# Scatter stage of a graph network kernel: GpSimd copies the next group's edge attributes in mid-group, in place of a wait for four scatters to land

## The reference

```
out_i = softplus(concat(x[i], edge_attr) @ W)      # (E, 4, 64)
out_j = softplus(concat(x[j], edge_attr) @ W)
alpha = softplus(sum(concat(out_i, out_j) * att))  # (E, 4)
alpha = softplus(batch norm of alpha over all edges)
alpha = softmax of alpha over the edges of one i
out   = mean over heads of segment_sum(out_j * alpha, i) + bias
x     = layernorm(x + out)
```

## Time and profile before

| | us |
|---|---|
| median of 3 runs | 7369.46 |
| lowest and highest | 7367.15, 7384.98 |
| the profiled execution, its own time | 7374.29 |
| the span of its profile | 7372.1 |
| mean granted TensorE clock | 0.861 |

### The profile page before, as it was taken

The page is one execution under the profiler, slowest core; times in us unless marked ns, Lnnn a source line. Parts: engine busy times, 40 slices in busy tenths (PEclk is TensorE's granted clock), DMA queues, the critical chain, the costliest instruction groups (busy, mean ns, idle before and its releaser), DMA issues. The chain is left out here.

```text
span 7372.1 us, 162457 instructions
## 1 busy us (share of the span) xinstructions
PE 5061.6 (69%) x33039; PEld 3158.5 (43%) x33040; DVE 5308.0 (72%) x27929; ACT 4071.5 (55%) x10690; POOL 2017.3 (27%) x2671
## 2 busy tenths in 40 slices
PE   1226766666666766637777777777724999995877
PEld 0113444344344443424444444444413555554877
DVE  5626666666666666629999999999987888887122
ACT  0015555455555555537777777777735889884000
POOL 0035555555655555541111111111100000000000
PEclk8557778778888778869999999999967999997978
DMA  4565555555555555555555555555514878773956
GB/s 33 219 226 166 178 165 177 169 165 178 170 177 168 171 174 164 172 175 144 144 145 145 144 146 144 144 145 145 144 34 121 214 213 222 213 214 103 381 225 258
DMA packets 905819, 1259.82 MB, mean 171 GB/s; under 512 B 267668, under 2 KB 774531, under 8 KB 884180
## 3 DMA queue, kind: packets, MB, share of 16 engines
q1 hardware_dynamic: 783812, 843.53, 41.2%
q0 software_dynamic: 88656, 333.99, 12.1%
q10 hardware_dynamic: 33216, 80.75, 3.2%
HBM read 832.07 MB, written 425.87 MB: 171 GB/s over the span
## 5 line engine op out<-in xcount | busy, mean ns | idle before, releaser
L840 POOL DMA_INDIRECT rows<-rowS,idx x1616 | 1605.0, 993 | 1151.7 <-DMA rows<-rowS,idx 605.1
L1530 DVE CUSTOM_DVE_ANT_1 junk<-bufh,attb 128x128 bf16<-128x128 f32 x7296 | 1693.7, 292 | 3.7 <-ACT bufh L1570 3.7
L1096 PE MATMUL psa<-one_c,one_s 128*128 128x392 bf16 x2352 | 651.4, 395 | 763.7 <-issue 322.7
L2219 PE MATMUL psm<-msg,onem 128*128 128x260 f32 x3648 | 1011.5, 402 | 135.1 <-issue 50.8
L989 ACT ACTIVATE lgS<-preS 128x1024 f32<-128x1024 f32 x404 | 412.7, 1021 | 893.0 <-remote 638.3
L2219 PEld LDWEIGHTS psm<-msg,onem 128*128 128x128 f32 x3648 | 619.1, 189 | 527.0 <-issue 473.0
L1502 POOL COPY eaC<-bufh 128x128 f32<-128x128 f32 x912 | 322.0, 353 | 1793.9 <-DMA bufh<-rows 1789.1
L923 DVE TENSOR_SCALAR one_c<-ioc,code 128x392 bf16<-128x392 f16 x2352 | 779.1, 331 | 18.3 <-DVE code L915 3.7
L1566 ACT ACTIVATE lg<-pre 128x512 f32<-128x512 f32 x912 | 544.9, 598 | 423.4 <-PE pre L1609 423.3
L2186 DVE TENSOR_TENSOR msg<-oj,alpha 128x512 f32<-128x512 f32 x912 | 631.1, 692 | 185.7 <-issue 96.7
L915 DVE TENSOR_SCALAR code<-pairS,codes 128x3 f32<-128x3 f32 x784 | 201.4, 257 | 782.2 <-remote 531.8
(11 more groups left out here) (275 smaller groups left out, 8107.7 us busy)
## 6 DMA issues: line engine op xcount, KB each, us to landing
bufh<-rows SPq DMA_DIRECT2D x912, 322.0 KB, 3.0
oj<-rows SPq DMA_DIRECT2D x912, 256.0 KB
adj<-adj SPq DMA_DIRECT2D x98, 1568.0 KB, 8.4
adj<-cnts ACTq DMA_DIRECT2D x49, 1568.0 KB
eaS<-in_edge_attr_dram SPq DMA_DIRECT2D x201, 256.0 KB
low<-dlow SPq DMA_DIRECT2D x202, 252.0 KB
rows<-fill POOLq DMA_DIRECT2D x20, 1610.0 KB
rows<-fill POOLq DMA_DIRECT2D x100, 322.0 KB
```

Of the source, the lines that this page charges most:

```text
L840: eng.indirect_dma_start(out=m["rows"][h], out_offset=bass.IndirectOffsetOnAxis(ap=idx[s][:, k:k + 1], axis=0), in_=rows[s][:, k, :], in_o ...
L1096: mm = eng.matmul(psa[r][:, 0:z.GC], one_s[r][:, k, :], one_c[r][:, k, :], start=(k == 0), stop=(k == GT - 1))
L1530: ins = eng.tensor_tensor_reduce(junk[q][:, k * H + h, :, :], buf[j][:, k, :, h * D:(h + 1) * D], attb[:, :, h, :], 1.0, 0.0, ALU.mult, AL ...
L2219: mm = eng.matmul(psm[j][:, 0:C + H], one[q][:, k, :], msg[q][:, k, :], start=(k == 0), stop=(k == UT - 1))
```

## The change

POOL gets a new function, `keep_ea`. It copies the edge attributes of a group from `eaS` into its row buffer, as ACT did at L1003, after the waits that ACT's copy had. POOL calls it for group 0 ahead of the loop, and then for group t+1 between the first and the second four scatters of group t. The wait of POOL for the first four scatters to land is gone. ACT's copy is gone with its two waits; the one on `sent` moves to the first softplus of the group, ahead of the Exp. SP still waits for `ea_kept` before it loads attributes into the same `eaS` buffer.

```
         @block.gpsimd
         def _(eng):
+            def keep_ea(b, s):
+                wait(eng, sent[s], b * 16 * K)
+                eng.wait_ge(ea_in[s % 2], ea_landed(b, s))
+                eng.sem_inc(begun, 1)
+                eng.tensor_copy(rows[s][:, :, C:C + D], eaS[s % 2][:, :, :]).then_inc(ea_kept, 1)
+
             def scatter(b, s, h=1):
...
-                    if part == 0:
-                        eng.wait_ge(sent[s], b * 16 * K + 16 * K // 2)
+                    if part == 0 and exists(*later(b, s, 1)):
+                        keep_ea(*later(b, s, 1))
...
+            keep_ea(0, 0)
             by_half(eng, blocks)
...
             def softplus(b, s, h):
                 t = step(b, s)
                 eng.wait_ge(pre_ready[h], t + 1)
                 wait(eng, out_ready[h], t)
+                if h == 0:
+                    wait(eng, sent[s], b * 16 * K)
...
                 eng.activation(eaT[s % 2][:, :, :], turned[:, :, :], ACT.Copy).then_inc(evacuated, 1)
-                wait(eng, sent[s], b * 16 * K)
-                eng.wait_ge(ea_in[s % 2], ea_landed(b, s))
-                eng.activation(rows[s][:, :, C:C + D], eaS[s % 2][:, :, :], ACT.Copy).then_inc(ea_kept, 1)
```

## The result

The changed kernel took 7555.2 us (median of four executions, 7547.5 to 7577.3) where the kernel before took 7368.3: a ratio of 1.0256, 95% interval 1.0227 to 1.0284. I had forecast 7312, with 7150 to 7480 as the range. That isn't the whole result. I measured the kernels again on five more chips, one after the other, and the measurements fall into two sets. In **set A** (the forecast's own measurement and the first two of these chips) the kernel before took 7368 to 7376 us. In **set B** (the last three chips) it took 7518 to 7534. In set B the same change makes the kernel 8.6% faster: 6873.6 us, ratio 0.9144, interval 0.9129 to 0.9159. Both sets have to be explained. I read set A first, since the forecast was made from it.

A forecast was written before the change was run, and what follows sets the result against it. SP, at half pace while POOL issues scatters, was taken as the bound. -0.35 - 0.05 + 0.15 = -0.25 us a group times 196 is -49 us, with -8 at the end -57: 7312 us, range 7150 to 7480.

The forecast's parts named there:

- What SP gets: SP's queue in the scatter stage: the landing wait returns as a wait for rows; -0.35 us a group, ends 0 and 0.8.
- T would stay at 13.56: Scatter stage: T, the time of a group, stays 13.56 us with SP at half pace in bursts, full pace outside.
- the second pause: POOL's some 1.0 us for the copy, besides 2.2 at the group's end; gives SP 0.4 to 0.5 us of work.
- SP at half pace: SP's loads in the scatter stage: 5.1 us of work done in POOL's 10.1 us of scatters; taken as the bound.
- VectorE's 753 us: VectorE's idle time ahead of `code`, steady part: 4.0 us a group, read as waiting for loads that SP issued late.
- The copy: Added on POOL, 128x512 f32: 0.7 us (0.35 to 1.41) plus 0.3 for the gap of an issue, 1.0 a group.
- ScalarE's relief: ScalarE loses 0.62 us a group, covered by its idle time; a little reaches SP: -0.05 us a group (0 to 0.1).
- The order in SP's queue: SP's load_ea waits for `ea_kept`, now set by POOL's copy: 0.3 us of stall, counted +0.15 us a group (0 to 0.8).
- the slower rival: SP's load_ea, every group: the wait for `ea_kept` stops SP; up to 0.75 us a group, 7392 to 7508 us; chance 0.28.
- The last groups: Last six groups, without pair loads: POOL sets the end; 12.85 us a group falls by 1.4 each, -8 us.
- POOL is the bound: Scatter stage follows POOL to 11.1 to 11.8 us a group, SP's slowness only elastic; -420, about 6950 us; chance 0.12.

## Why the prediction was wrong

**The step that failed** is in "What SP gets": "T would stay at 13.56" when the landing wait goes. That POOL's pauses add up to T - 10.1 only says what T is made of; that T itself stays had no row behind it. In set A taking out the wait alone costs 14.70 - 13.56 = 1.14 us a group, and in set B it gives back 14.26 - 10.50 = 3.76. I had priced that removal at nothing and the second pause at -0.35. A pause that comes back is a symptom: it is the time in which POOL waits for late rows, and it comes after the delay and not ahead of it.

**The bound** was misread with it. I took SP at half pace for the capacity that limits the stage. In set A SP got more time to wait and the stage got slower. Half of what I saw was right (SP is slow while POOL issues, there); that it bounds was an inference from small waits, and PE's late signals I had not looked for. In the rows of before they stood as "remote". There I also misread a row: of VectorE's 753 us ahead of `code` only 179.9 are put down to loads of pairs (1.0 us a group and not 4.0), and 510.4 to "remote".

**The copy** was taken at 0.7 us and took 0.63; with its gap I had 1.0, and it costs 0.49 us (set A's timeline) to 0.57 (11.07 - 10.50 in set B). By the Trainium skill's rule on the port shared with VectorE ("SBUF — State Buffer", section "Who interferes with whom") I had allowed a hold of 0.33 us more. The traces show a hold, on both sides. Copies with nothing on VectorE beside them never took over 634 ns. Beside VectorE's work they took up to 882 ns in the changed kernel of set A, and up to 1109 in the kernel with the wait ahead of the copy, where 46 of 202 took over 800. VectorE pays as well: in the changed kernel its `one_s` (L931) takes 249 ns as a rule, and 661 (medians) in the 119 cases that overlap a copy. No sum of mine had that term. It can't be what makes set A's loss, which comes without any copy on POOL.

**ScalarE's relief** (-0.05) can't be seen in set A, where the change and the deleted wait alone have the same time. **The order in SP's queue** (+0.15, to 0.8): SP waits 0.6 us for `ea_kept` in the changed kernel, and opening this loop gave nothing. So the slower rival had the sign and not the mechanism.

**The last groups:** in set A the last 48 scatters take 73.6 us (starts at 3379.8 and 3453.4), 12.3 us a group where it was 12.85. I had expected 1.4 us less for each group, and it was 0.6.

**The rival "POOL is the bound"** is the outcome of set B. It gave 11.1 to 11.8 us a group, and it is 11.07. Its time (about 6950) lies 76 us above the measured 6873.6, since it took 11.45 us a group. That the ratio came out as far down as 0.9144 is luck for this rival: in set B the kernel before stands at 14.26 us and not 13.56, since its waits cost 4.17 us. I had tied this rival to the Trainium skill's rule that DMAs issued by SP never touch GpSimd's descriptor path and are immune to interference there ("DMA: Bandwidth & Descriptors", section "SWDGE vs HWDGE vs iDMA"). I had read too much into it: the interference that it speaks of is VectorE's hold of the shared port, and that POOL's scatters can't slow SP was my own extension. Set B fits the extension (SP's move takes 29 ns in 560 of 560), set A doesn't (up to 1389 ns), and neither speaks against the rule. The text before said what would make it wrong: that SP's slowness depends on something other than POOL's issuing. It does, or at least on something beside it: both sets have the issuing.

**What stays open** is what makes set A. The later measurements ran each on another chip and set A's came first, so chip and hour aren't told apart. What I dismissed too easily is the recording. I had written that profiled and unprofiled runs agree within 5 us, so that the slowness is real; but each timed execution comes with a span and a granted clock too, so it was recorded in some way as well, and the comparison says nothing. In set A the trace of the kernel before holds 72,330 updates of semaphores, in set B 106,090, for the same 162,457 instructions. All ten traces of set A hold 70,956 to 73,340 such updates, and nine of set B 104,418 to 106,090 (the tenth, with half the scatters, 95,562). Of the 33,760 that the kernel before lacks in set A, 31,177 are landings of DMAs. The missing ones all belong to the scatter stage: from 800 to 2800 us there are 7.8 a microsecond in set A and 19.5 in set B, while from 3600 to 5200 us, in the stage after it, both have 11.9. The Trainium skill ("NOTIFIC — Programmer's Manual", section "When the ring fills") says that a full queue of event records loses new ones, overwrites old ones or stalls the engine that made them, as it is set. Records are lost in set A; that the recording also holds PE's signals and SP up would fit, and no run here shows it. It might as well be the delay that loses the records.

Not tried: the pause at the group's end and the memset of 2.7 us in set A, since each time that they ran it was in set B. So whether a pause at another place, or as long as the landing wait, would do in set A is open.

## What to carry over

A wait that looks superfluous may be the only pause that other engines get. Before pricing its removal at nothing, take out that wait alone, and replace it by an idle fill of growing length: the time and the period of these kernels give the answer that a trace of before can't. Look at the same kernel on more than one chip before trusting a sign: here 2.6% slower and 8.6% faster are the same change. If a time has to hold in both conditions, keep the wait and put the copy inside it (0.9987 and 0.9559); if only the second one counts, leave the wait out and the copy where it was (0.8973).

## What was unexpected in the hardware

- In set A, while POOL issued scatters without a pause, two engines that waited for a finished product of PE went on 9.6 us after its end, 2.0 us after the burst's end; in set B, under denser issuing, ScalarE went on after 0.12 us (product ended at 1445.01, ScalarE began at 1445.13).
- A copy on POOL beside VectorE's work: up to 1109 ns for the copy where it takes 611 to 634 alone, and 661 ns in place of 249 for VectorE's `one_s` that overlaps it.
- Scatters of 8 in place of 322 floats a row: nearly the same period in set A (14.58 against 14.70 us).
- The same kernel, 162,457 instructions, differs by 1.9 to 2.2% between the sets, and the ranking of its variants turns round.
